# VectorE makes the low halves of the query features before it chooses the experts of the group one round back

## The reference, cut to what matters

```python
xn = layernorm(x)
neigh_mean = segment_sum(xn[src], dst) / deg
h = xn @ W_self.T + neigh_mean @ W_neigh.T + bias        # then layernorm, gamma, beta
q, k, v = split(xn @ w_qkv.T)                            # 8 heads of 64
q = elu(q * 64**-0.5) + 1;  k = elu(k) + 1
out = (q @ (k.T @ v)) / (q @ k.sum() + 1e-8)             # per head
x2 = x + gnn + (out @ w_out.T + b_out)
t = layernorm(x2)
hs = gelu(t @ sw1.T + sb1) @ sw2.T + sb2                 # two shared experts
top_v, top_i = top_k(softmax(t @ gate_w.T + gate_b), 2)  # the choice of the experts
y = x2 + hs + sum over the two chosen experts of top_v * expert(t)
```

## Time and profile before

| | |
|---|---|
| timed executions, median (lowest, highest) | 2492.79 us (2492.04, 2495.35) |
| the profiled execution: span | 3045.0 us |
| busy: PE / PEld | 2386.2 (78%) / 1485.9 (49%) |
| busy: DVE / ACT / POOL | 1527.7 (50%) / 1097.3 (36%) / 1284.0 (42%) |
| mean granted TensorE clock | 0.863 of full speed |
| group stage, from the first to the last L1883 | 480.3 to 2305.2 us |

### The profile page before, as it was taken

One profiled execution on the slowest core, in us unless ns is written; L12 is line 12 of the kernel. 1 busy time (PEld: TensorE's weight loads), 2 busy tenths in 40 slices (PEclk: granted clock), 3 DMA queues, 4 the chain that ended last, 5 costly groups with the idle time before them and its releaser, 6 DMA issues. The chain is left out here.

```text
span 3045.0 us, 46892 instructions
## 1 busy us (share of the span) xinstructions
PE 2386.2 (78%) x13332; PEld 1485.9 (49%) x13333; DVE 1527.7 (50%) x3736; ACT 1097.3 (36%) x2118; POOL 1284.0 (42%) x1370
## 2 busy tenths in 40 slices
PE   5989868767777777777777777777785899988999
PEld 3545434444444444444444444444453666665776
DVE  7889733444444444434344433444465344444666
ACT  3556633323333333333232333333341344332333
POOL 4656755444443444434444444444420232223443
PEclk9999968788887788877787887888786999999999
DMA  8466456555444455444555544545434454546776
GB/s 284 149 211 201 150 151 179 169 152 150 146 142 134 141 150 151 149 137 144 150 152 152 152 141 148 152 146 155 143 118 152 139 160 158 159 147 198 255 256 212
DMA packets 190001, 497.26 MB, mean 163 GB/s; under 512 B 42012, under 2 KB 54812, under 8 KB 188152
## 3 DMA queue, kind: packets, MB, share of 16 engines
q0 software_dynamic: 92720, 309.47, 35.0%
q1 hardware_dynamic: 66505, 135.52, 13.2%
q10 hardware_dynamic: 30719, 51.60, 4.5%
HBM read 373.91 MB, written 122.50 MB: 163 GB/s over the span
## 5 line engine op out<-in xcount | busy, mean ns | idle before, releaser
L614 POOL DMA_INDIRECT region<-table,ebuf x225 | 230.8, 1026 | 571.6 <-DMA ebuf<-edges 492.6
L614 POOL DMA_INDIRECT Wff<-table,ebuf x225 | 222.4, 988 | 364.9 <-DMA ebuf<-edges 302.9
L323 PE MATMUL bank<-Wff,region 128*125 128x512 f16 (+1 forms) x636 | 264.5, 416 | 132.4 <-issue 66.5
L654 POOL DMA_INDIRECT region<-table,idx x122 | 116.8, 957 | 360.5 <-PE bank L1298 267.7
L324 PE MATMUL bank<-Wff,region 128*125 128x512 f16 (+1 forms) x636 | 260.2, 409 | 0.0
L325 PE MATMUL bank<-Wff,region 128*125 128x512 f16 (+1 forms) x636 | 258.3, 406 | 0.0
L1137 PE MATMUL bank<-region,ohs 128*125 128x512 f16 x850 | 232.6, 437 | 16.3 <-issue 16.0
L1137 PE MATMUL bank<-Wff 128*125 128x512 f16 x850 | 215.8, 413 | 16.7 <-issue 15.8
L621 POOL DMA_INDIRECT region<-table,ebuf x200 | 192.7, 963 | 60.9 <-issue 60.9
L1871 DVE SCALAR_TENSOR_TENSOR region<-bank,sv,bias_bc 125x512 f32<-125x512 f32 x50 | 37.5, 749 | 359.3 <-remote 224.0
L621 POOL DMA_INDIRECT Wff<-table,ebuf x200 | 191.7, 958 | 60.9 <-issue 60.9
(11 more groups left out here) (322 smaller groups left out, 5822.3 us busy)
## 6 DMA issues: line engine op xcount, KB each, us to landing
yd<-region ACTq DMA_DIRECT2D x59, 512.0 KB, 3.1
x2d<-region SPq DMA_DIRECT2D x25, 512.0 KB, 3.8
table<-region SPq DMA_DIRECT2D x25, 512.0 KB
region<-x2d SPq DMA_DIRECT2D x25, 512.0 KB
table<-region POOLq DMA_DIRECT2D x50, 250.0 KB, 3.4
xnt<-region POOLq DMA_DIRECT2D x25, 500.0 KB, 4.0
region<-xnt SPq DMA_DIRECT2D x25, 500.0 KB
x2t<-region SPq DMA_DIRECT2D x25, 500.0 KB
```

The lines of the kernel that those rows point to most:

```text
L323: wmm(ps, xh, wh, start=first, stop=False)
L614: pool.indirect_dma_start(out=ring[j][:, s, :], out_offset=None, in_=table, in_offset=bass.IndirectOffsetOnAxis(ap=ebuf[j][:, 2 * s:2 * s ...
L654: pool.indirect_dma_start(out=tg[:, c, :], out_offset=None, in_=table2, in_offset=bass.IndirectOffsetOnAxis(ap=idx[:, 2 * turn + c:2 * tur ...
```

## The change

In VectorE's `group`, `gate(prev)` and the loop that makes the low halves change places. No operation is added, removed or altered; the instructions of the other engines are as they were.

```diff
@@ VectorE, group(i, prev, nxt)
                     for k in range(2):
                         stt(qe[:, 2 * c + k, :], ... ALU.mult, ALU.mult).then_inc(sem["q_hat"], 1)
-                if prev is not None:
-                    gate(prev)
                 for c in range(2):
                     cc = slice(2 * c, 2 * c + 2)
                     dve.wait_ge(sem["q_hi"], 2 * i + c + 1)
                     tt(qh[:, 1, cc, :], qe[:, cc, :], qh[:, 0, cc, :], ALU.subtract).then_inc(sem["q_lo"], 1)
+                if prev is not None:
+                    gate(prev)
                 if nxt is not None:
                     halved(nxt, 1)
```

## The result

The changed kernel takes 2574.83 us (median of 4 runs, 2571.43 to 2578.72). The kernel before took 2493.26 us in the same comparison (4 runs, 2492.04 to 2495.35). The ratio is 1.0325, with a 95% interval of 1.0312 to 1.0337. The change makes the kernel slower by 81.6 us; the forecast was 56 us slower. The direction and most of the mechanism were right, and the loss was sized a third too small.

The account below looks back on a forecast made before the run. Two chains of nearly equal length, VectorE's to the mean and TensorE's through the queries, were taken to bound each round. 1.2 us delay plus 1.24 clock, 2.44 over 23 rounds, gave 56.1 us and 2549; range 2504 to 2578.

Parts of the forecast that it names:

- The attention product starts 2.43 us earlier: TensorE, group round: low halves done sooner, so the attention product, `places` and the queries each move 2.43 us earlier.
- VectorE does not win it and loses 1.40: VectorE, gate to mean: gate starts 1.40 us later, `halved`'s register loads lose their cover, so `halved` and mean come 1.40 later.
- L1127 comes 1.2 us later, because TensorE's loads are bare: TensorE behind L1195: register loads exposed once it waits for the mean; L1127 1.2 us later, taken between 1.0 and 1.4.
- the second case of the prediction's third step: TensorE at L1127: if only some 7 attention matmuls run at the lower clock, the queries end sooner and L1127 loses 1.4 us.
- The clock costs 1.24 a round: TensorE, `aggregate(i, 1)`: gaps around L1195 lower the clock; 1.24 us a round, three quarters of 1.65, between 0 and 2.32.
- The rival that the clock falls in every round: TensorE, `aggregate(i, 1)`: full clock loss in all 23 rounds, 23 x (1.2 + 2.32) = 81 us, giving 2574; chance 0.10.
- What would show it: Profile signs: L1690 1.7 us behind L1804, attention product at 3.2, L819 at 18.6, L1127 behind 1.4, `aggregate(i, 1)` near 10.
- the wait is simply gone: TensorE's wait before the attention product: VectorE's chain not last, loads free, 2.43 us a round gained, 2435 us; chance 0.11.

Follow-up runs that it names:

- bare_loads: Kernel before, gate still first, with VectorE made to wait for its low halves before the register loads of `halved`: 2545.57 us, ratio 1.0221.
- second profile: The kernel before profiled again with no edit, without the idle stretches of its first profile: 2492.88 us, profiled span 2491.3 us.
- fill_gap: pe_loads_after plus twelve matmuls with overwritten results ahead of L1195, to keep TensorE at work: 2495.75 us, ratio 1.0009 against the kernel before.
- both_loads: Changed kernel with VectorE's register loads of `halved` directly behind the low halves and TensorE's of `aggregate(i, 1)` ahead of L1195: 2494.77 us, ratio 1.0008.
- mean_early_after: Changed kernel with the next group's first mean moved early, directly behind the low halves on VectorE and ahead of ScalarE's one-hot rows: 2507.23 us, ratio 1.0080.
- all: both_loads with the early first mean of mean_early_after: 2514.91 us, ratio 1.0085 against the kernel before.
- loads_under_low: Changed kernel with VectorE's two register loads of `halved` issued directly behind the low halves, ahead of the gate: 2573.37 us, ratio 1.0321 against the kernel before.
- pe_loads_before: Kernel before with TensorE's two register loads of `aggregate(i, 1)` issued behind the queries, ahead of L1195: 2492.76 us, ratio 0.9997.
- pe_loads_after: Changed kernel with TensorE's two register loads of `aggregate(i, 1)` issued behind the queries, ahead of L1195: 2510.95 us, ratio 1.0068 against the kernel before.

## Why the prediction was right, and where its size was off

**The attention product starts 2.43 us earlier.** Right: 2.64 in the mean (6.23 to 3.59). The queries end 2.35 earlier.

**VectorE does not win it and loses 1.40.** Right, and the term best supported. `halved` starts at 7.84 in place of 6.44, and the mean ends 1.44 later. (The 1.40 is made of a gate that starts 1.30 later and takes 0.17 longer, and of 0.07 less between L1804 and L1690.) `bare_loads` shows the cause alone: the same 1.65 us of idle time and a mean 1.28 later, with the swap left out.

**L1127 comes 1.2 us later, because TensorE's loads are bare.** The size was nearly right, 1.42 measured; the reason was right in part. Round 23 had been taken for a timed round, and in it the loads run under the queries. In the loop rounds of the second profile they were bare before, too: L1127 stood 1.99 us behind L1195 in the mean, against 0.53 in the earlier trace rows. After, it is 2.80. What did not move is the distance from the mean to L1127, 2.87 before and 2.85 after. So the loss is simply the mean's delay, passed on in full, and not loads that become bare. That is the second case of the prediction's third step (1.4); it took 1.2 between its two cases, and that this came near is in part luck.

**The clock costs 1.24 a round.** This is the term that was mis-sized: `aggregate(i, 1)` runs 1.75 longer and starts 0.29 later behind L1127, 2.04 together. The mean row said 1.65, and I cut it by a quarter, on the ground that some of the falls belonged to disturbed queries. It should not have been cut: the clock fell in all 20 rounds (8.92 to 9.63, never 7.55). The gap in front of the matmuls was put at 1.8 us up to 3.2 plus 1.4 for the loads; it is 2.80 plus 1.95. `fill_gap` shows that the first part is the cause where the loads are covered, and `bare_loads` that a small one is enough where they are not; in the changed kernel itself neither was taken away alone. The rival that the clock falls in every round (2574) came nearest to the measured time. What it says of the clock is what happened; its sum, 1.2 + 2.32, has both terms off (1.42 and 2.04), and that they cancel to 1 us is luck.

The page of the Trainium skill "TensorE: Matmul & The Clock Gate", section "HAM oscillation — how this bites in real kernels", says that a wait between bursts of matmuls that is long enough lets the gate go back to half rate, so that the next burst starts cold. The rows of `aggregate(i, 1)` agree after the change. Before the change it stood behind shorter idle times, 0.70 to 1.95 us, and stayed at 7.55 in all 20 rounds. A wait by itself does not decide it.

**Sum.** 2574.83 lies inside the stated range, 3 us below its upper end. A round, 2.44 foretold against 3.55: 0.22 of the difference in L1127's delay, 0.80 in the clock, 0.09 elsewhere.

**What would show it.** L1690 stands 1.65 behind L1804, nearly all idle (1.7 foretold). Round 23 of the changed kernel starts at 1774.59, its attention product at 1777.81, 3.22 later (3.2 foretold), and L819 ends 1792.48 + 0.69 - 1774.59 = 18.58 behind the start (18.6). L1195 stands there behind a wait of 1.75 us, L1127 behind 1.17 (1.4), and `aggregate(i, 1)` takes 10.03 us (near 10):

```profile
1792.48 0.69 ACT L819 ACTIVATE region<-bank,dg 125x512 f32<-125x512 f32 x1 [12.65 <-issue]
1793.31 0.62 PE L1195 MATMUL bank<-ident,region 125*128 125x125 f32 x4 [1.75 <-ACT region L819]
1795.10 0.68 PE L1127 MATMUL bank<-zeros 1*125 1x512 f16 x1 [1.17 <-issue]
```

Over the whole span L1195 waits for L819 23 times, 63.7 us in all (21 times and 38.4 us in the earlier trace rows, not once in the second profile of the kernel before); the idle time at the loads of both engines is listed below it:

```profile
PE bank L1195 <- ACT region L819: 63.7, 23, 3.8
DVE Wff L1690 <- issue: 68.6, 48, 1.6
PEld bank L1127 <- issue: 64.3, 50, 2.6
```

**What the prediction did not see** is the second chain. The rival "the wait is simply gone" put 58 us on the table. No run found them. VectorE's second mean ends at 30.52, and TensorE needs it at 31.46, less than 1 us later. In `both_loads`, `fill_gap` and `mean_early_after`, which have the low halves first, it ends at 31.29 to 31.55, and from the second turn a round takes 23.1 to 23.3 us more. These three all come out at 54.65 to 54.94 a round, however early their first `aggregate(i, 1)` is. `all` has its second turn as early and takes 55.48, so the second mean is not the whole of it.

## What to carry to other kernels

An operation that stands in front of a register load may be its cover. Before moving it, ask what will lie over the load then, on every engine that loads a loop bound: here 1.3 us of work moved by one place cost 1.4 us on VectorE and, through the mean, as much on TensorE. The wait of the busiest engine that was shortened here moved to its next input, and there the lower clock came on top of it; look first for the next thing the engine will wait for, and the one behind that. Where a profiled execution is longer than the timed ones, take another before trusting one quiet round in it.

## What the runs showed of the hardware

- The same register load takes from 0.30 to 1.8 us within one execution, and its median differs between executions. TensorE's of L1123 (ns min/median/max) in the kernel before, second profile, against a median of 303 in the earlier trace rows, and in the changed kernel:

```profile
L1123 PEldq TENSOR_LOAD <-rounds x50: 298/678/1832, 384.3 to 1714.2; - x50
```

```profile
L1123 PEldq TENSOR_LOAD <-rounds x50: 297/838/1822, 384.2 to 1793.4; - x50
```

The other load of the pair, L1124, goes the other way: its median is 618 ns in the first profile of the kernel before and 302 and 304 in these two. What makes a load long was not tested.

- Work that is thrown away can make the kernel faster: 12 more matmuls a round, 15 us less.
- Time freed ahead of TensorE's bursts was twice given back by the clock. In `loads_under_low` the start of `aggregate(i, 1)` won 0.46 us and its length lost 0.57; in `pe_loads_before` the attention product came 0.43 earlier and ran 13 matmuls at the lower clock in place of 9. Only `bare_loads` separates the rounds by their gap. In `pe_loads_after` the clock fell behind gaps of 1.84 to 3.78 us in 19 rounds and held behind 2.73 and 3.01 in two, so the length of the gap alone does not decide it; what else does stays open.
